# A post-norm attention and feed-forward layer on one core: another order and other banks for the next q, the turnings of h and the first context

## The reference

```python
q = (x @ Wq + bq); k = (x @ Wk + bk)[:, None]; v = (x @ Wv + bv)[:, None]   # q in 16 heads
q, k = _rotary(q, HD), _rotary(k, HD)
attn = softmax(q @ k.T / sqrt(HD));  ctx = attn @ v                          # per sequence and head
x = _layernorm(x + (ctx @ Wo + bo))
h1, h2 = x @ quantize(w1).T, x @ quantize(w2).T                              # 512 -> 1408, weights -1, 0, 1
x = _layernorm(x + (sigmoid(h1) * h2) @ quantize(w3).T)
```

## Time and profile before

| what | us |
|---|---|
| median of 3 runs | 621.79 |
| lowest and highest run | 616.76 and 622.9 |
| the profiled execution | 620.83 |
| span of its instructions | 619.0 |
| around the span | 1.8 |
| mean granted TensorE clock | 0.961 of 2.4 GHz |

### The profile page before, as it was taken

How to read it: one execution, slowest core, us unless ns; L and a number is a source line. 1 busy time by engine, 2 the same in 40 slices (tenths; PEclk the granted TensorE clock), 3 DMA queues, 4 the chain that set the end, 5 groups by cost and what they waited for, 6 DMA issues and landing times.

```text
span 619.0 us, 9143 instructions
## 1 busy us (share of the span) xinstructions
PE 550.4 (89%) x2964; PEld 272.5 (44%) x2964; DVE 469.6 (76%) x635; ACT 426.8 (69%) x865; POOL 302.8 (49%) x398
## 2 busy tenths in 40 slices
PE   5778878888978999999899999999599999989993
PEld 2454454424433443445444444454344444444441
DVE  1867876747997988988989998799979898435432
ACT  1697787727796888777898887687978898134310
POOL 1308798887655433778565423978464310211001
PEclk9799979987998999999999999999799999999997
DMA  8490534027999799799999996999997999200001
GB/s 298 133 352 6 163 132 161 1 64 148 188 179 207 149 179 163 141 180 179 218 207 211 184 180 127 180 181 193 175 214 148 181 163 195 69 1 35 0 1 68
DMA packets 217103, 92.12 MB, mean 149 GB/s; under 512 B 204384, under 2 KB 205536, under 8 KB 216544
## 3 DMA queue, kind: packets, MB, share of 16 engines
q1 hardware_dynamic: 209952, 77.61, 60.9%
q0 software_dynamic: 6144, 12.60, 9.9%
q10 hardware_dynamic: 960, 1.33, 0.6%
HBM read 20.20 MB, written 4.19 MB: 39 GB/s over the span
## 4 chain that ended last, share of the span: by engine, by line
PE 60%; DVE 13%; issue 8%; ACT 8%; DMA 5%; POOL 2%; SPq 2%; POOLq 0%; ACTq 0%; DVEq 0%
PE a_ps L1245 12%; PE b_ps L1245 6%; PE c_ps L1337 6%; PE s_ps L1258 5%; PE e_ps L1245 5%; PE s_ps L1285 5%; PE a_ps L1176 5%; DVE p_all L1005 4%; PE b_ps L1258 3%; PE c_ps L1323 3%; DMA pt_sb<-p_all 2%; DVE sh_sb L998 2%; DMA late<-in_w 2%; ACT p_all L709 2%; PE b_ps L1230 2%
## 5 line engine op out<-in xcount | busy, mean ns | idle before, releaser
L709 ACT ACTIVATE p_all<-s_ps,sh_sb 128x512 f32<-128x512 f32 x192 | 130.2, 683 | 70.9 <-DVE sh_sb L998 69.8
L998 DVE TENSOR_REDUCE sh_sb<-s_ps 128x2 f32<-128x1024 f32 x96 | 116.6, 1215 | 27.6 <-PE s_ps L1285 27.5
L1005 DVE SCALAR_TENSOR_TENSOR p_all<-p_all 128x1024 f16<-128x1024 f32 x96 | 131.2, 1366 | 3.3 <-ACT p_all L717 3.1
L717 ACT ACTIVATE p_all<-p_all 128x1024 f16<-128x1024 f32 x96 | 101.7, 1059 | 2.0
L1245 PE MATMUL a_ps<-late,q 128*128 128x512 f16 x352 | 85.1, 385 | 3.9 <-ACT th L680 2.3
L1285 PE MATMUL s_ps<-k_st,q_st 128*128 128x512 f32 x192 | 80.7, 501 | 8.0 <-ACT p_all L709 4.6
L417 POOL DMA_DIRECT2D q_st<-hi x96 | 49.5, 518 | 62.3 <-ACT hi L643 37.1
L540 POOL TENSOR_SCALAR rstd<-mv 128x1 f32<-128x1 f32 x32 | 8.6, 270 | 136.0 <-DVE mv L965 135.9
L1176 PE MATMUL a_ps<-xT_sb,wq_sb 128*128 128x512 f32 x104 | 55.8, 669 | 10.0 <-DMA wq_sb<-in_wq 6.2
L1245 PEld LDWEIGHTS a_ps<-late,q 128*128 128x128 fp8e4 x352 | 32.1, 99 | 47.6 <-issue 9.1
L417 POOL DMA_DIRECT2D q_st<-lo x96 | 47.4, 498 | 9.1 <-DVE lo L908 8.7
(11 more groups left out here) (147 smaller groups left out, 1005.9 us busy)
## 6 DMA issues: line engine op xcount, KB each, us to landing
q_st<-hi POOLq DMA_DIRECT2D x96, 64.0 KB, 3.4
q_st<-lo POOLq DMA_DIRECT2D x96, 64.0 KB, 4.0
late<-in_w SPq DMA_DIRECT2D x2, 2816.0 KB, 11.2
xT_sb<-in_xT SPq DMA_DIRECT2D x8, 512.0 KB, 5.5
late<-in_x SPq DMA_DIRECT2D x4, 1024.0 KB, 6.4
out<-late SPq DMA_DIRECT2D x12, 256.0 KB, 2.9
late<-in_w SPq DMA_DIRECT2D x2, 1408.0 KB, 6.9
q_st<-hi SPq DMA_DIRECT2D x32, 64.0 KB, 2.1
```

Source lines behind the costliest of these rows:

```text
L709: act.activation(p_pair[n][:, t % 2, :], pair_banks(h * PAIRS + t // 2)[:, t % 2, :], ACT.Exp, bias=sh_sb[:, 2 * n + t % 2:2 * n + t % 2 + ...
L717: act.activation(p_half[n][:, 0, :], p_pair[n].rearrange("p t k -> p (t k)"), ACT.Copy, scale=P_SCALE).then_inc(p_hi, 1)
L998: dve.tensor_reduce(sh_sb[:, 2 * n:2 * n + 2], pair_banks(h * PAIRS + i), AX.X, ALU.min).then_inc(maxed, 2)
L1005: dve.scalar_tensor_tensor(out=p_half[n][:, 1, :], in0=p_pair[n].rearrange("p t k -> p (t k)"), scalar=P_SCALE, in1=p_half[n][:, 0, :], op ...
```

## The change

PE's table has another order from k = 8 to k = 13. The first turning of h comes a step earlier, beside `wo3`; the next q comes before the other three turnings and before the score of step 10; turnings 1 and 2 stand together at k = 10; the first context comes a step earlier, and turning 3 behind it; `sums0` is a step ahead of `up0`. The q of sequences 2 and 3 goes to bank b, and turning 1 to bank a. ACT and DVE take the halves of h in the new order: `h_high` 0 at k = 8, 1 and 2 at k = 10, 3 at k = 11; `h_low` 0 at k = 9, 1 and 2 at k = 11, 3 at k = 12. In body 3 the empty row of the table moves with q0 from 10 to 9.

```diff
     [("wo2", -1)],
-    [("wo3", -1)],
-    [("ht0", -1), ("ht1", -1)],
+    [("wo3", -1), ("ht0", -1)],
     [("q0", 1)],
-    [("ht2", -1), ("ht3", -1)],
-    [("ctx0", 0)],
-    [("sums0", 0), ("up0", -1)],
+    [("ht1", -1), ("ht2", -1)],
+    [("ctx0", 0), ("ht3", -1)],
+    [("sums0", 0)],
+    [("up0", -1)],
...
-LAST_BESIDE = {10: [], 25: [("wa0", 0), ("sums2", 0)], 26: [("da0", -1)], 27: [("db0", -1)], 28: [("dc0", -1)],
+LAST_BESIDE = {9: [], 25: [("wa0", 0), ("sums2", 0)], 26: [("da0", -1)], 27: [("db0", -1)], 28: [("dc0", -1)],
...
     if kind == "ht":
-        return [("abeb" if s == B - 1 else "ebeb")[n]]
+        return [("abeb" if s == B - 1 else "eaeb")[n]]
...
     if use[0] == "q":
-        return ["e" if use == "q3" and s else "a"]
+        return ["e" if use == "q3" and s else "b" if use == "q0" and s > 1 else "a"]
...
                         h_rows(s, (6, 7, 9, 10).index(k))
-                    if k == 9:
+                    if k == 8:
                         h_high(s, 0)
+                    if k == 9 and b < B - 1:
+                        unit(b + 1, "q0")
+                    if k == 10:
                         h_high(s, 1)
-                    if k == 10:
-                        if b < B - 1:
-                            unit(b + 1, "q0")
+                        h_high(s, 2)
                     if k == 11:
-                        h_high(s, 2)
                         h_high(s, 3)
...
-                    if k == 10:
+                    if k == 9:
                         h_low(s, 0)
+                    if k == 11:
                         h_low(s, 1)
+                        h_low(s, 2)
                     if k == 12:
-                        h_low(s, 2)
                         h_low(s, 3)
```

## The result

| | median us | runs | lowest and highest |
|---|---|---|---|
| before | 619.27 | 4 | 616.53 and 622.9 |
| changed | 630.14 | 4 | 628.73 and 631.62 |

The ratio is 1.017, with a 95% interval of 1.0113 to 1.0226: the change makes the kernel slower, by 10.9 us in the medians. The profiled execution took 629.36 us, 8.5 more than that of before. (The kernel before was run again beside the experiments; its median came out between 616.7 and 619.9 there, and single runs between 612.6 and 626.2.) All ratios here are taken to runs of before of the same time and leave out its slower state, so that they are not quotients of the medians beside them.

The account below looks back on a forecast made before the run. PE was taken to bound most stretches, so a shift of up0's start shifts the end. From 620.83 us profiled, less 0.8 at full clock, plus 4.8 for the clock, came 624.8, taken as 624.5; range 617 to 630, eight in ten.

Parts of the forecast that it names:

- The hold: p_low of pair 11 starts 0.15 us behind POOL's L518 in each body and waits 1.0 us for it.
- The first rival: p_low of pair 11, starting ahead of L518, is held by two POOL instructions: 1.2 us more per body, 628.4; chance 0.17.
- E: Moment when ACT begins exps of pair 10; after the change up0 was to start at E + 10.75 us.
- The load of x in body 2: q0, now before score 10, waits 2.2 us for the next x, making exps of pair 10 1.7 us later.
- (c): q0 no longer waits 1.86 us for its bank, held by the fourth attended; the gain is spent on the load wait.
- E in bodies 1 and 3: The earlier h_low 0 on DVE delays exps of pair 10 by 0.3 us in body 1, 0.4 in body 3.
- The clock: Half-clock stretches before up0, on body 2's q0 and in body 3 add 4.8 us; bounds -1.7 to +6.5.
- The 1.4 us for a late p_low in body 3: Slow ctx0 in body 3 lets score 12, not exps of pair 10, set p_low, costing 1.4 us.
- ctx0 a step earlier: First context waits 1 to 2 us for its transposing DMA, but score 12 stays early enough: price 0 at full clock.
- the move of `sums0` off the path: At the end of the chain to up0, sums0 no longer stands on the path; no separate size given.
- Bodies 1 and 3 at full clock: up0 was to start 1.9 us earlier in body 1 and 1.0 us earlier in body 3.
- The second and third rivals: Second: p_low ahead of POOL, clock never falls, 615.3, chance 0.14. Third: change moves nothing, 620 to 622, chance 0.19.

Follow-up runs that it names:

- Experiment 1: Changed kernel, with POOL's three rotation instructions of q3 waiting until the p_low of pair 11 is done: 622.33 us, ratio to before 1.0081.
- Experiment 7: Changed kernel, POOL's rotations waiting for p_low of pair 11, two unread matmuls ahead of up0: 619.40 us; with next x also loaded a step earlier: 615.36 us.
- Experiment 6, PE filled: Changed kernel with four matmul calls of unread result ahead of up0 in each body: 623.26 us, ratio to before 1.0057.
- experiment 9: Changed kernel with the first context back behind turning 3 and score 12, and sums0 back beside up0: 625.47 us, ratio to before 1.0128.
- the early load: SP issues the load of the next x one step earlier (k == 6 for k == 7); alone on the changed kernel: 629.37 us, ratio to before 1.0205.
- control of number 3: Kernel before, with the load of the next x issued one step earlier: 619.13 us, ratio to before 1.0031.
- both: Changed kernel with POOL's q3 rotations waiting for the p_low of pair 11 and the next x loaded a step earlier: 621.41 us, ratio to before 1.0056.
- POOL's wait alone: Changed kernel, with only POOL's q3 rotations made to wait for the p_low of pair 11: 622.33 us, ratio to before 1.0081.

## Why the prediction was right and wrong

The forecast was 624.5 us, slower by 0.4%, with "within 1%" as the likeliest; it is slower by 1.7%, and 630.14 lies 0.1 us over the upper end of the range of 617 to 630. On the scale of the profiled execution, on which the sum was made, it is 629.36, just inside. The chain of causes was right in nearly every link; two sizes were too small, the hold and the load.

- **The hold, forecast at 1.0 us in each body: wrong size.** This is the term that failed: "By that row the wait costs 1.0 us, and `p_low` ends at L518 + 2.35". The place was exact: the p_low began 0.15 and 0.14 us behind L518 in bodies 1 and 2, forecast 0.15. But it was held by two instructions, 2.2 us, for which I had a row as well, 183.45 in body 1, of the same p_low at the same place, and I took the one at 260.69 because its order was the same. The first rival, at 0.17, had the size and not the condition: it wanted the p_low ahead of L518, and it came behind. `up0` came at E + 12.0 in all three bodies; forecast was E + 10.75, the rival says 12.0. Experiment 1 shows that the hold sets `up0`. The rival's time of 628.4 compares with 629.36 in the profiled execution, which is partly luck: the three windows grew by 10.5 us where the rival's sum has 7.6, and the stretches between gave 2 us back.
- **The load of x in body 2: right in kind, short in size.** Forecast was a wait of 2.2 us and E later by 1.7 at full clock. The wait was 3.14, as the load was issued 0.5 us later behind score 8 than before and took 0.5 us longer, landing at 8.4 us instead of 7.4, while PE was there at 5.4 and not 5.2; and q0 fell on half clock, which I had in the clock term with 1.7. E came at 15.7 us behind score 8 for 11.1 before: 4.6. Experiment 7 puts the price of the late load at 4 to 6 us. (The bank that q0 waited for in the kernel before was freed by the fourth `attended`, as the prediction says under (c), not by the third.)
- **E in bodies 1 and 3**: forecast +0.3 and +0.4, measured +0.7 and +0.8. Score 9 stands behind `ht0` now and made `row_max` 9 about 0.3 us late, which I had left out; in body 1 the load made PE wait 0.6.
- **The clock, forecast at +4.8: right in size.** `up0` fell on half clock in all three bodies (I had taken two), q0 of body 2 too, and body 3 behind score 10 as well. From `up0` to score 14 the three bodies lost 4.1 us against before. q0 of body 2 took 5.37 us where 3.6 is usual, 1.8 more; it had done so before as well (5.40), but behind score 10. That makes 5.9, within the bounds of -1.7 to +6.5. The 1.4 us for a late p_low in body 3 did not come: it started at E + 8.6 and was held for less. Experiment 6 gets back 6.9 us by keeping PE busy.
- **"ctx0 a step earlier ... Price 0 at full clock."** The condition was the point. Its move takes 3.6 us of work out of the gap before `up0`; experiment 9 puts the price of this move and that of `sums0` at 4.7 us by the medians, 2.6 by the ratios. The clock term had the cost, but not its cause, and I had counted the move of `sums0` off the path as a gain.
- **Bodies 1 and 3 at full clock, 1.9 and 1.0 earlier**: 0.2 earlier and 0.5 later behind score 8. The missing 1.2 of the second POOL instruction and the late E account for it, in body 3 too: `up0` lies 12.0 us behind E there as well, so the slow context added nothing.
- **The second and third rivals** fell: nothing got ahead of POOL, the clock did fall, and `up0` of body 2 moved by 6.2 us.

What stays open: why a p_low is held by two POOL instructions here and by one at 260.69, with the same start behind L518 to 0.2 us. There it ran between L518 and L521, and L521 waited:

```profile
260.38 1.27 POOL L518 TENSOR_TENSOR rot<-raw,table_sb 128x512 f32<-128x512 f32 x1
261.60 2.27 POOL L521 TENSOR_TENSOR rot<-rot,table_sb 128x512 f32<-128x512 f32 x1
```

It is not chance: in all fourteen profiled kernels the p_low of that place is held by one instruction (2.01 to 2.04 us), and the p_low of pair 11, wherever it was held, by two. One difference that the rows show is what POOL did just before: L547 there, DMA issues here; nothing was run to test it. Also open is whether it is chance that the profiled kernels with the changed order and the early load spend 165.9 to 167.4 us before score 8 of body 1, where the control of number 3 has 164.8 (others without the early load lie between 164.0 and 166.7).

## What to carry to other kernels

When a dependent step is moved, write down which instruction of another engine it will stand beside, to a tenth of a microsecond; here a p_low that started 1.35 us ahead of L518 (before, body 2) took 1.21 us, and one that started 0.14 us behind it took 3.44. Of two rows that could price a meeting, take the one of the same instruction at the same place, not the one whose order looks neater. And work that fills a wait of PE is not free to move: here the gap that it left was paid for in the clock of what came next.

## What the runs showed of the hardware that was not expected

- The p_low of pair 11, with both inputs in SBUF, was held through the first two of POOL's three 1.27 us instructions whenever it started between 0.57 us before L518 (before, body 1: 4.17 us) and 1.07 us after it (PE filled, body 3: 2.53). That is 17 meetings in seven kernels, and it ended 3.58 to 3.63 us behind the start of L518 in every one, ahead of L524, which then took 2.13. At 0.83 us before L518 (control of number 3, body 1) it was not held, and L518 took 1.54.
- At another place the p_low got through. At about 140 us, where POOL had been idle ahead of L518, a p_low that started 0.18 to 0.63 us before it took 1.22 us in all fourteen profiled kernels, and L518 took 1.72 to 2.17. An `h_low`, with one input in PSUM, was not held in any: 0.69 us at most.
- Twelve matmul calls whose result nobody reads made the kernel 6.9 us faster. After an idle stretch of PE of 3.7 to 4.3 us the granted clock stood at 0.5, 1.2 GHz, in some part of `up0` (0.55, 0.50 and 0.57 in the mean of its first 3.3 us) in all three bodies of the changed kernel; after idle stretches of 2.1 us it did so in bodies 1 and 3 of "both" but not in its body 2, nor in body 1 with POOL's wait alone. Part of the scatter of this kernel, 612.6 to 626.2 us before, may be that; it was not tried.
